# A quarter of the next batch's state scan moved from the attention heads to the Q and K products

## What is computed

```
x   = in_proj_w @ ctx ; u = silu(conv4(x) + b)
x_dbl = x_proj_w @ u  -> dt_lo (16), B (16), C (16)
delta = softplus(dt_proj_w @ dt_lo + bias)
for each step l, channel e, state n (512 x 512 x 16):
    state = state * exp(delta * A[n]) + (delta * u) * B[n]
    y    += state * C[n]
y = (y + D * u) * silu(layernorm(rows))
rows = rows + tanh(g0) * y
q, k, v = rms(layernorm(rows)) @ wq, wk, wv ; q, k rotated (rope)
ctx = softmax(causal(q k^T / sqrt(32))) @ v ; residual, norm, router
```

## Time and profile before

| | us |
|---|---|
| median of three runs (lowest, highest) | 1934.68 (1929.93, 1940.09) |
| the profiled execution's own time | 1934.3 |
| its span, first to last instruction | 1932.5 |
| first round (batch 0's scan), from 0 | 199.6 |
| mixed rounds: 199.6 to 465.4, to 733.8, to 1000.0 | 265.8, 268.4, 266.2 |
| last attention alone, 1000.0 to about 1198 | 198 |
| mixture of experts, to the end | 734 |
| busy in the span: PE, DVE, ACT, POOL | 1549.7, 1179.2, 887.3, 810.2 |

### The profile page before, as it was taken

The page is one execution under the profiler, slowest core; times in us unless marked ns, Lnnn a source line. Parts: engine busy times, 40 slices in busy tenths (PEclk is TensorE's granted clock), DMA queues, the critical chain, the costliest instruction groups (busy, mean ns, idle before and its releaser), DMA issues.

```text
span 1932.5 us, 26585 instructions
## 1 busy us (share of the span) xinstructions
PE 1549.7 (80%) x9104; PEld 1184.7 (61%) x9104; DVE 1179.2 (61%) x1730; ACT 887.3 (46%) x1973; POOL 810.2 (42%) x809
## 2 busy tenths in 40 slices
PE   5246877777967778777769776899999999999995
PEld 2234545555635556445546444778888799999974
DVE  4689658887588886589863332333232566656545
ACT  4433446664366663466641563121211466666510
POOL 0595146552255541365522121144321455555544
PEclk8555976888967898868889687999999999999997
DMA  5620000210101111011101102822120577777464
GB/s 197 231 77 22 23 11 29 61 45 28 39 22 50 55 34 39 6 34 46 46 25 60 64 30 72 320 84 86 55 71 1 191 249 259 247 250 260 156 233 157
DMA packets 92373, 191.54 MB, mean 99 GB/s; under 512 B 8704, under 2 KB 25600, under 8 KB 88912
## 3 DMA queue, kind: packets, MB, share of 16 engines
q1 hardware_dynamic: 87120, 173.07, 26.2%
q0 software_dynamic: 5120, 16.78, 2.6%
HBM read 136.21 MB, written 53.61 MB: 98 GB/s over the span
## 4 chain that ended last, share of the span: by engine, by line
PE 42%; DVE 5%; issue 5%; ACT 3%; POOL 3%; DMA 0%; DVEq 0%; ACTq 0%; SPq 0%; POOLq 0%
PE scores L528 21%; PE bank L528 12%; PE scores L647 2%; POOL yab L1933 2%; PE bank L675 1%; PE bank L592 1%; PE bank L660 1%; DVE YA L1382 1%; ACT EX L1037 1%; PE bank L825 1%; DVE HS L1372 1%; ACT PT L1045 1%; PE scores L650 1%; DVE nm L1424 1%; ACT bank L1002 1%
## 5 line engine op out<-in xcount | busy, mean ns | idle before, releaser
L1782 POOL TENSOR_TENSOR GB<-DU,BB 128x512 f32<-128x512 f32 x256 | 327.8, 1294 | 125.7 <-DVE HS L1372 67.6
L592 PE MATMUL bank<-ident,HS 128*128 128x128 f32 x896 | 185.1, 342 | 173.0 <-DVE YA L1382 118.2
L1372 DVE TENSOR_TENSOR_SCAN HS<-bank,GB 128x512 f32<-128x512 f32 x224 | 273.4, 1220 | 47.8 <-ACT bank L1002 23.9
L592 PEld LDWEIGHTS bank<-ident,HS 128*128 128x128 f32 x896 | 125.1, 172 | 222.5 <-DVE YA L1382 157.3
L1002 ACT ACTIVATE bank<-DL,aneg 128x512 f32<-128x512 f32 x224 | 154.9, 692 | 131.8 <-DVE HS L1372 130.5
L1382 DVE SCALAR_TENSOR_TENSOR YA<-bank,Ct,YA 128x512 f32<-128x512 f32 x224 | 164.6, 735 | 28.6 <-PE bank L592 26.3
L1045 ACT ACTIVATE PT<-bank 128x128 f32<-128x128 f32 (+3 forms) x256 | 110.5, 432 | 112.8 <-PE bank L660 111.5
L528 PE MATMUL scores<-xth,wgh 128*128 128x256 f32 x552 | 158.2, 287 | 2.4 <-DVE fa L1668 1.3
L528 PE MATMUL scores<-xth,wgl 128*128 128x256 f32 x552 | 156.3, 283 | 0.0
L528 PE MATMUL scores<-xtl,wgh 128*128 128x256 f32 x552 | 156.2, 283 | 0.0
L660 PE MATMUL bank<-ident,EX 128*128 128x128 f32 x640 | 129.7, 310 | 27.8 <-ACT PT L1045 26.0
(11 more groups left out here) (243 smaller groups left out, 3823.7 us busy)
## 6 DMA issues: line engine op xcount, KB each, us to landing
wgr<-wffn_in SPq DMA_DIRECT2D x108, 384.0 KB, 6.4
wdr<-wffn_in SPq DMA_DIRECT2D x81, 256.0 KB, 3.1
BB<-b_scratch SPq DMA_DIRECT2D x64, 256.0 KB, 3.2
xg<-V SPq DMA_DIRECT2D x1, 11776.0 KB, 40.5
xr<-xg SPq DMA_DIRECT2D x23, 512.0 KB, 5.7
yg<-ysb SPq DMA_DIRECT2D x23, 512.0 KB, 6.4
hah<-hhd SPq DMA_DIRECT2D x5, 1024.0 KB, 6.0
hal<-hhd SPq DMA_DIRECT2D x5, 1024.0 KB, 8.1
```

The costliest lines, as they stand in the source:

```text
L592: mm = nc.tensor.transpose(state_bank(s, q)[:, et * P:(et + 1) * P], HS[:, n % 2, et, tt * P:(tt + 1) * P], ident[:])
L1372: nc.vector.tensor_tensor_scan(HS[:, n % 2, et, :], decay_bank(s, k), GB[:, k % 4, :], 0.0, ALU.mult, ALU.add).then_inc(scan_done, 1)
L1782: nc.gpsimd.tensor_tensor(GB[:, k % 4, :], DU[:, et, :], BB[:, n % 2, :], ALU.mult).then_inc(gb_ready, 1)
```

## The change

The core of the diff (the names' new lines differ from those of before by up to 80):

```diff
+SQ = 16
+SU = 3
...
+        even_states = arena(sh)("even_states", [P, T4, L])
+        sh.close()
         w_in = mid("w_in", [P, DC // P, DI])
+        cT = mid("cT", [P, DC // P, L])
...
-        HS = arena(sh)("HS", [P, 2, T4, L])
...
+        ZT = XR = EX
...
+        def states(s, n):
+            return xa[:, s % 2] if n % 2 else even_states
+
         def state_bank(s, q):
-            return (HT0, A[0])[q % 2] if s == 0 else HT0
+            if q >= NB - T4:
+                return (HT0, PB)[q % 2], q - 1 if s and q == NB - T4 else q - 2
+            if s == 0 or q < SQ - T4:
+                return (HT0, A[2])[q % 2], q - 2
+            return HT0, q - 2 if q == SQ - T4 else q - 1
 
         def decay_bank(s, k):
-            return (HT1, A[1])[k % 2] if s == 0 else HT1
+            if s == 0 or k < SQ:
+                return (A[3], HT1)[k % 2], k - 2
+            return HT1, k - 1
...
             def load_ctx(s):
-                at(sp, xp_mm, T4 * s)
+                at(sp, hT_ready, NB * s - T4)
+                sp.dma_start(w_in[:], w_in_in).then_inc(scanw_in, 16)
                 sp.dma_start(cT[:], ctx_in[s]).then_inc(ctx_in_s, 16)
+            def load_residual(s):
+                sp.wait_ge(z_done, T4 * s + T4)
+                at(sp, t_mm, UN * s)
+                for i in range(T4):
+                    sp.dma_start(XR[:, i, :], x_in[s][:, i, :]).then_inc(x_ld[s % 2][i], 16)
...
             def product(b, m):
                 if m < 2:
                     at(pe, lg_done, T4 * b)
+                    if b + 1 < B:
+                        pe.wait_ge(dt_abs, T4 * (b + 2))
+                        pe.wait_ge(dt_rel, T4 * (b + 2))
+                        pe.wait_ge(yi_done, T4 * (b + 1) + 3)
...
                 if q == 0:
                     pe.wait_ge(v_done, T4 * b + T4)
                     pe.wait_ge(qk_done, 8 * b + 8)
+                    if b + 1 < B:
+                        pe.wait_ge(scan_done, NB * (b + 1) + SQ)
+                        pe.wait_ge(y_acc, NB * (b + 1) + SQ - T4)
...  (PE, round_)
                 for m in range(8):
                     if att:
                         product(b, m)
                         if m:
                             rotate(b, m - 1)
-                    if scn:
-                        if m < 2:
-                            du_term(s, 2 * m)
-                            du_term(s, 2 * m + 1)
-                        if m == 2:
-                            turn_c(s)
-                        if 2 <= m < 6:
-                            delta(s, m - 2)
+                    if scn and m >= 2:
+                        turn_states(s, 2 * m - 4)
+                        turn_states(s, 2 * m - 3)
...
-                        if scn and q:
-                            turn_states(s, T4 * (q - 1) + a)
+                        if scn and a < SU:
+                            turn_states(s, SQ - T4 + SU * q + a)
...
-                    for q in range(NB - T4, NB):
-                        turn_states(s, q)
-                    for tt in range(T4):
-                        turn_z(s, tt)
+                    turn_z(s, 0)
+                    turn_z(s, 1)
+                    turn_states(s, NB - 4)
+                    turn_states(s, NB - 3)
+                    turn_z(s, 2)
+                    turn_states(s, NB - 2)
+                    turn_states(s, NB - 1)
+                    turn_z(s, 3)
...  (ACT)
             def decay(s, k):
                 n, et = blocks(k)
+                into, before = decay_bank(s, k)
...
-                if k > (s == 0):
-                    act.wait_ge(scan_done, NB * s + k - (s == 0))
+                if before >= 0:
+                    act.wait_ge(scan_done, NB * s + before + 1)
...
                     xdbl(s)
+                    y_start(s, 0)
+                    y_start(s, 1)
                     for rt in range(T4):
                         z_rows(s, rt)
                     for rt in range(T4):
                         z_tanh(s, rt)
+                    for et in range(T4):
+                        delta_abs(s, et)
+                    delta_exp(s)
+                    y_start(s, 2)
+                    y_start(s, 3)
+                    for et in range(T4):
+                        delta_log(s, et)
+                    decay(s, 0)
+                    keep_c(s)
+                    decay(s, 1)
                 for m in range(8):
                     if att:
                         bias(b, m)
                     if scn:
...
+                        decay(s, 2 * m + 2)
+                        if m < 7:
+                            decay(s, 2 * m + 3)
...  (DVE)
+            def scan_block(s, k):
+                scan(s, k)
+                if k >= T4:
+                    add_state(s, k - T4)
...
+                for m in range(8):
+                    if scn:
+                        scan_block(s, 2 * m)
+                    if att:
+                        rope_out(b, m)
+                    if scn:
+                        scan_block(s, 2 * m + 1)
...  (POOL)
-                if att:
-                    for m in range(8):
+                for m in range(8):
+                    if att:
                         rope_cos(b, m)
+                    if scn:
+                        driven(s, 2 * m)
+                        driven(s, 2 * m + 1)
```

More of the change, by code:

```diff
@@ L719, in round_ @@
                     finish(b - 1, T4 - 1, 2)
+                if scn:
+                    xdbl(s)
+                    du_term(s, 0)
+                    du_term(s, 1)
                 if att:
                     values(b, 2)
+                if scn:
+                    delta(s, 0)
+                    delta(s, 1)
+                if att:
                     values(b, 3)
                 if scn:
-                    xdbl(s)
+                    delta(s, 2)
+                    delta(s, 3)
+                    du_term(s, 2)
+                    du_term(s, 3)
+                    turn_c(s)
                 for m in range(8):
@@ L1162, in round_ @@
                         finish(b, i - 1, m + 1)
-                    if scn and k + 4 < NB:
-                        decay(s, k + 4)
+                    if scn and k + SU < NB:
+                        decay(s, k + SU)
                     if s == 0 and q % 2 and q // 2 < KC:
@@ L1465, in round_ @@
                     conv(s, 1)
+                if att and scn:
+                    z_stats(s, 0, 3)
                 if att:
@@ L1522, in round_ @@
                     if scn:
-                        scan(s, k + 3)
-                    if scn and q:
-                        add_state(s, k - 1)
+                        scan_block(s, k + 2)
                     if more:
@@ L1533, in round_ @@
                 if scn:
-                    for q in range(NB - T4, NB):
-                        add_state(s, q)
                     scan_out(s)
@@ L1863, in round_ @@
                         finish(b, i - 1, 1)
-                    for a in range(2):
-                        if scn and k + a < NB:
-                            driven(s, k + a)
+                    if scn and k < NB:
+                        driven(s, k)
                     if att:
@@ L1870, in round_ @@
                         context(b, q - 1)
-                    for a in range(2, 4):
+                    for a in range(1, SU):
                         if scn and k + a < NB:
```

227 lines of the change are left out of this document (119 added, 108 removed).

## The result

| | before | after |
|---|---|---|
| median of the runs, us | 1933.33 | 2015.68 (2014.88 to 2016.12) |
| ratio, 95% interval | | 1.043 (1.0415 to 1.0446) |
| span of the profiled execution | 1932.5 | 2013.9 |
| busy PE, DVE, ACT, POOL | 1549.7, 1179.2, 887.3, 810.2 | 1560.5, 1174.1, 887.6, 808.3 |

(1933.33 is the median of the runs beside those of the change.) The change is slower by 82 us, where +36 was forecast and the range ended at 2000. The direction was right, the size was not, and none of the rivals gives such a time. PE's busy time grew by 11, the other engines' not at all: nearly all of it is waiting.

What follows compares the result with a forecast made beforehand. DVE was taken to pace the first three groups of heads, less surely the fourth. The terms -84 + 113 + 21 - 10.5 - 3 - 1 = +36 on 1934.3 gave 1970 us, range 1922 to 2000.

Steps and rivals of the forecast that it cites:

- A: Attention heads of the mixed rounds: one scan block fewer per quad saves 28 us a round, -84 in three.
- B: Way to a mixed round's first bias: 8.7 us longer, first bias at 245.5 instead of 236.8.
- C: Q and K products' stage: a chain through four engines, 8.5 us a step; with B, +113 over three rounds.
- The clock's term: Q and K products' stage: PE work partly slowed by a lower clock, 7 us a round, +21 in three.
- The rival of the low clock: Products' stage: PE stays at its lower clock throughout, 15.5 us a round, 1996 in all; chance 0.16.
- D: Scan ends: 3.5 us shorter per mixed round, -10.5 in three, and -3 in the first round.
- E: First round: chain into its first scan some 6 us shorter, but a B row's load holds it; -1 taken.
- F: Second load of a round's rows and reload of weights and context: covered by other work, cost 0.
- The tight coupling: Heads: one block less lets coupled quads fall towards their floors, 39.5 us less a round, 1914 in all; chance 0.11.

Runs made afterwards that it cites:

- e14: Changed kernel; in the mixed rounds' heads decays no longer wait for scans, nor turned states for additions, operands' memories kept: 1936.92 us.
- e15: Kernel before the change, four blocks a quad, with the same two waits cut as in e14: 1875.53 us.
- e16: Changed kernel; in the heads turned states no longer wait for additions, but decays still wait for scans: 1992.66 us.
- e1: Changed kernel; in the products' stage ACT issues a step's two decays one block later and POOL computes inputs ahead of rope_cos: 1996.55 us.
- e2: Changed kernel with e1's edits, and PE turns the states of a step's second block a step later: 1972.5 us.
- e18: Changed kernel, whole computation kept; the heads' decays in four SBUF buffers and turned states in two banks: 1966.62 us.
- e17: The edits of e18 on the changed kernel without scan blocks among the products (four a quad in the heads), whole computation kept: 1904.33 us.
- e5: Changed kernel; the heads' additions read gate rows in SBUF instead of the bank, and PE waits for none of them: 1999.16 us.

## Why the prediction was wrong, and where it was right

**A failed.** "The heads shed a block per quad: 28 per round." They shed 8.1, 9.3 and 10.4, below even the lower bound of 12.7. The step took DVE's busy share for the pace and priced a block at DVE's 2.05. Two things were wrong in it.
- The heads stood in two circles of waits, each through one PSUM bank: decay and scan between ACT and DVE, turned states and addition between PE and DVE. Attention's copies, exponentials and transposes stand in the same queues. With the work unchanged, cutting both gives 26 a round, cutting one 3 or 7. The change left both circles as they were, one bank each. The prediction read the 0.18 of waiting on DVE before a scan, where the wait is small, and not the waits on the other side, 32.3 on PE and 26.6 on ACT.
- A block is not worth DVE's two operations even without the circles: 16 a round (e14, e15), not 28. Halving the scans gave 11 for 23 of DVE's time.

The bound below, 12.7, spread the cost of the scan evenly over its blocks; that a block could be worth less than its share, since the circles stay however few blocks go through them, was left out. How the 9 are made up, operation by operation, stays open. The granted clock of the heads rose from 0.76 to 0.85 with both cuts, and PE's busy time fell from 122.5 to 107.8 for the same 920 matmuls; so some of the 26 comes through the clock. The runs don't part it from the waits; but e16 had 0.82 and 114.7 and shed only 7, so the clock alone doesn't bring it.

**B held.** The first bias was forecast at 245.5 and came at 243.61, 45.5 into the round for 45.9. The first scan came 49.2 and 52.7 into the round ("near 49").

**C held.** A step of 8.5 was forecast (7.8 for the first two), and 8.1, 7.6 and then 9.5 to 8.4 were measured, the decays waiting for scans in the rows above. e1 and e2 undid the order by parts and gained 19 and 43.

**The clock's term** was too large. B and C put the first row maximum 37.8 later at full clock, and the term added 7; measured are 42.0, 41.0 and 41.1 in the three rounds. That leaves 10.7 in sum, where 21 were forecast, and only as far as B and C are exact. In the first round 2.8 of its 4.2 are the four waits for PE's rotation above. The rival of the low clock, with 15.5 a round, falls as a mechanism, though the total went beyond its 1996. The rule of the Trainium skill that spoke for this rival, "TensorE: Matmul & The Clock Gate", The HAM clock gate, is borne out in its direction alone: the stage that ran at 0.94 was granted 0.80 from the first bias to the first row maximum (243.6 to 316.2), where PE was busy 40.8 of 72.6 us. It lost a part of its clock as it thinned out, and did not stay at the lower level.

**D held** in the mixed rounds (-10.6 for -10.5). **D and E** in the first round gave -1.5 for -4. **F held**: between 199 and 1084, in the mixed rounds, no engine of the kernel after is shown waiting for a load, and what comes behind those rounds moved by 2.9.

The tight coupling was among the rivals, but the other way round: it was to make the heads shed more than DVE's 2.05 a block. The coupling is there, and it makes them shed less.

## What to carry to other kernels

Before pricing work taken from a busy engine, read the waits of the *other* engines for it: here PE and ACT waited some 30 us each for an engine that was 86% busy, the stage was held by hand-overs, and taking work away brought a third to a half of its duration. Two single buffers that are handed between three in-order engines can hold each other's gains back: cut or double them together, or the trial of one alone (3 and 7 us here) hides what both are worth (26). In an experiment that cuts a wait, keep each operand in its memory, and run the by-products of a large change alone: here they were the gain.

## What the runs showed of the hardware

A DVE operation with both tensors in SBUF and POOL's two-input operation beside it slow each other. A scan took 1.22 with its factor in PSUM and 1.51 to 1.60 with it in SBUF (e18, e17), an addition 0.74 and 0.87 (e5); POOL's inputs went from 1.28 to 1.82 and 1.92, though nothing of theirs was edited. That it takes both engines at once shows in the heads of e18's three mixed rounds: the 23 scans from SBUF with no POOL instruction beside them took 1.20 to 1.23, as from PSUM, and the 117 with one beside them for more than a moment 1.62 on average and up to 2.35; POOL's inputs took 1.27 without such a scan beside them and 1.87 with one. The Trainium skill, "SBUF — State Buffer", SBUF: two separate sides, says that a VectorE operation with two SBUF inputs and a GpSimd operation that reads SBUF lock one pair of ports in turn, for the whole instruction. The runs agree that both sides pay, +0.33 and +0.35 on DVE and +0.54 to +0.63 on POOL on average; they don't show which of them held the ports. It cost e17 the whole of what its second bank had won.
